# Two attentions and a mixture of experts in one kernel: the steady step's work in another order

## The reference

```python
# layer A: 16 heads of width 8 on ONE shared key and value head, causal, rotary
q = (x @ Wq + bq).reshape(Bx, Tx, 16, 8); k = (x @ Wk + bk)[:, :, None, :]; v = (x @ Wv + bv)[:, :, None, :]
q, k = rope(q), rope(k)
att = softmax(where(causal, -inf, einsum('bthd,bThd->bhtT', q, k) / sqrt(8)))
x = layernorm(x + einsum('bhtT,bThd->bthd', att, v).reshape(...) @ Wo + bo)
# layer B: 16 query heads and 4 key and value heads of width 64, causal, rotary
n = rmsnorm(x, g1); q, k, v = n @ wq, n @ wk, n @ wv ...
h = x + softmax(mask(q k) / 8) v @ wo
# and a mixture of 8 experts (top 2, with a capacity), each gelu((x w2) * (x w1)) w3
x = layernorm(x + h + moe(rmsnorm(h, g2), router_w, router_b, w1, w2, w3))
```

## Time and profile before

| what | value |
|---|---|
| median of the runs | 568.52 us |
| the profiled execution | 569.94 us, of which the span (first to last instruction) 568.1 |
| mean granted TensorE clock over the span | 0.957 of full speed |
| PE busy | 474.3 us (83%), 2980 matmul instructions |
| weight loads busy | 262.4 us (46%) |
| DVE busy | 373.4 us (66%) |
| ACT busy | 231.3 us (41%) |
| POOL busy | 161.9 us (28%) |
| one reduce of a maxima tile on DVE, L1340, mean | 686 ns |
| one copy of a bank by ACT, L1972, mean | 595 ns |

### The profile page before, as it was taken

How to read it: one execution, slowest core, us unless ns; L and a number is a source line. 1 busy time by engine, 2 the same in 40 slices (tenths; PEclk the granted TensorE clock), 3 DMA queues, 4 the chain that set the end, 5 groups by cost and what they waited for, 6 DMA issues and landing times.

```text
span 568.1 us, 8434 instructions
## 1 busy us (share of the span) xinstructions
PE 474.3 (83%) x2980; PEld 262.4 (46%) x2980; DVE 373.4 (66%) x1023; ACT 231.3 (41%) x418; POOL 161.9 (28%) x200
## 2 busy tenths in 40 slices
PE   3877877899899999999998999899888689798730
PEld 2445443454455455536454554455436236465520
DVE  3634789667666786585867577776966136745585
ACT  1252431744554274338334642642431330545332
POOL 4311222402402243033313132232332760051612
PEclk9986999999999999999999999999988789999985
DMA  7400000000030003001100300030430350041213
GB/s 213 168 2 2 1 2 1 2 1 1 3 77 2 0 3 77 1 3 36 42 1 4 76 2 0 5 76 1 141 86 10 106 161 1 1 133 32 64 53 97
DMA packets 19095, 23.95 MB, mean 42 GB/s; under 512 B 2630, under 2 KB 15374, under 8 KB 18158
## 3 DMA queue, kind: packets, MB, share of 16 engines
q1 hardware_dynamic: 15308, 18.29, 11.9%
q0 software_dynamic: 1648, 4.07, 2.6%
q10 hardware_dynamic: 2098, 1.05, 0.6%
HBM read 16.81 MB, written 6.28 MB: 41 GB/s over the span
## 4 chain that ended last, share of the span: by engine, by line
PE 57%; DVE 19%; ACT 11%; issue 6%; POOL 3%; another core or an unknown queue 2%; DMA 1%; ACTq 1%; POOLq 0%; DVEq 0%
PE ps_r L997 6%; PE ps_st L962 6%; PE ps_r L867 5%; DVE rmax_a L1340 4%; ACT pt L1902 4%; PE ps_r L712 4%; PE ps_r L1024 4%; PE ps_st L1242 4%; PE ps_st L951 4%; PE ps_r L1013 3%; PE ps_r L770 3%; DVE rmax L1340 3%; PE ps_r L844 2%; POOL qkr L603 2%
## 5 line engine op out<-in xcount | busy, mean ns | idle before, releaser
L603 POOL TENSOR_TENSOR qkr<-qkr,prod 128x512 f32<-128x512 f32 (+1 forms) x48 | 52.3, 1095 | 191.6 <-DVE prod L1466 190.5
L1340 DVE TENSOR_REDUCE rmax_a<-ps_r 128x2 f32<-128x512 f32 (+1 forms) x96 | 61.2, 686 | 31.2 <-PE ps_r L844 31.0
L1340 DVE TENSOR_REDUCE rmax<-ps_r 128x2 f32<-128x512 f32 (+1 forms) x96 | 60.7, 684 | 13.5 <-PE ps_r L976 13.1
L1902 ACT ACTIVATE pt<-ps_st 128x1024 f32<-128x1024 f32 x48 | 46.5, 1022 | 54.7 <-PE ps_st L754 54.6
L712 PE MATMUL ps_r<-cbt 128*128 128x256 bf16 (+1 forms) x192 | 61.9, 323 | 4.0 <-ACT xT_b L1926 1.1
L1911 ACT ACTIVATE pt<-ps_st 128x1024 f32<-128x1024 f32 x48 | 47.3, 1022 | 37.0 <-PE ps_st L962 31.6
L997 PE MATMUL ps_r<-pt,vb 128*64 128x512 f32 x192 | 50.0, 627 | 7.7 <-issue 4.2
L640 POOL TENSOR_TENSOR oT<-pvb,oT 128x1024 f32<-128x1024 f32 x14 | 32.9, 2371 | 78.9 <-DMA oT<-inv_dram 78.9
L1024 PE MATMUL ps_r<-wqkv,xT_b 128*128 128x512 f32 x96 | 44.5, 600 | 4.3 <-DVE rmax_a L1340 3.5
L712 PEld LDWEIGHTS ps_r<-cbt 128*128 128x128 bf16 x192 | 18.6, 97 | 48.0 <-issue 34.6
L962 PE MATMUL ps_st<-qbuf,kbuf 64*128 64x512 f32 x288 | 39.8, 408 | 0.0
(11 more groups left out here) (238 smaller groups left out, 888.9 us busy)
## 6 DMA issues: line engine op xcount, KB each, us to landing
oT<-inv_dram SPq DMA_DIRECT2D x14, 512.0 KB, 5.7
xs_dram<-pvb SPq DMA_DIRECT2D x1, 2048.0 KB
pt<-in_L_ffn_w SPq DMA_DIRECT2D x2, 1024.0 KB, 7.1
ys_dram<-qkr SPq DMA_DIRECT2D x14, 128.0 KB
qkr<-xs_dram POOLq DMA_DIRECT2D x4, 256.0 KB, 7.0
x_all<-in_L_attn_x ACTq DMA_DIRECT2D x1, 896.0 KB, 7.2
pvb<-xs_dram POOLq DMA_DIRECT2D x3, 256.0 KB, 3.9
out<-x_all SPq DMA_DIRECT2D x1, 640.0 KB
```

The source lines that it names most:

```text
L603: nc.gpsimd.tensor_tensor(part, part, prod[:, (3 * t + i) % 2, 0:w], ALU.add).then_inc(add_in, 1)
L1340: nc.vector.tensor_reduce(heads_of(i), ps_r[:, b, :].rearrange("p (h k) -> p h k", h=4 if i < 4 else 2), AX.X, ALU.max).then_inc(free[b], 1)
L1902: nc.scalar.activation(pt_a(kind)[:, 8 * half:8 * half + 8, :], ps_st[:, c % 2, :, :].rearrange("p b (h t) -> p (b h) t", h=4), ACT.Exp, s ...
```

## The change

The order of a step is another one on all engines, and the ring's list with it; no operation is added or taken away. In PE's stream: `turn_values` and bm0 come ahead of `scores(s, 0)`; the maxima tiles of A and B alternate singly in places; the output projection's two tiles are separated by am6, and stand before bx and bv2; the projection's thirds stand singly between maxima tiles, p12 behind `values_a(s, 0)`; layer A's input is turned earlier; `turn_qk` is split into thirds with `project_a` and `turn_tokens` between. DVE and ACT follow: ACT takes bv3 before the first exponentials of A, DVE rotates p00, p01 and p02 between reduces, and does two splits before `rotate_a`. SP issues the row of nm1 before the sums. Step 7 gets a function of its own on each engine (`last_step`), with the order that it had. The diff, cut (left out are the loops over `range(lo, hi)` in `rotate`, `split` and `high_parts`, and the same calls with all thirds in the opening steps):

```diff
--- before.py
+++ after.py
@@ -68,23 +68,19 @@
 NCH = len(CHUNKS)
-ORDER = [("TA", "tv0"), ("TA", "tv1"), ("MA", "am0"), ("MA", "am1"), ("MB", "bm0"), ("MB", "bm1"),
-         ("TA", "ot0"), ("TA", "ot1"), ("SB", "bv0"), ("MA", "am2"), ("MA", "am3"), ("TA", "ao0"), ("TA", "ao1"),
-         ("MB", "bm2"), ("MB", "bm3"), ("SB", "bv1"), ("SB", "sm0"), ("MA", "am4"), ("MA", "am5"),
-         ("MB", "bm4"), ("MB", "bm5"), ("SB", "bv2"), ("MA", "am6"), ("MA", "am7"), ("MA", "nm0"), ("PB", "bx"),
-         ("TB", "bo0"), ("TB", "bo1"), ("MA", "am8"), ("MA", "am9"), ("MB", "bm6"), ("MB", "bm7"),
-         ("PB", "p00"), ("PB", "p01"), ("PB", "p02"), ("MA", "am10"), ("MA", "am11"), ("SB", "bv3"), ("MA", "nm1"),
-         ("SB", "sm1"), ("MB", "bm8"), ("MB", "bm9"), ("MB", "bm10"), ("MB", "bm11"), ("PB", "p10"), ("PB", "p11"),
-         ("PB", "p12"), ("MB", "nmT"), ("PA", "ax"), ("SA", "av0"), ("PA", "qkv"), ("TB", "xfT"),
-         ("PB", "r00"), ("PB", "r01"), ("PB", "r02"), ("TB", "lg"), ("PB", "r10"), ("PB", "r11"), ("PB", "r12"),
-         ("SA", "av1"), ("PA", "qT0"), ("PA", "qT1"), ("PA", "kT0"), ("PA", "kT1")]
+ORDER = [("TA", "tv0"), ("TA", "tv1"), ("MB", "bm0"), ("MA", "am0"), ("TA", "ot0"), ("TA", "ot1"), ("SB", "bv0"),
+         ("MA", "am1"), ("MA", "am2"), ("MB", "bm1"), ("MA", "am3"), ("SB", "bv1"), ("SB", "sm0"), ("TA", "ao0"),
+         ("TA", "ao1"), ("MB", "bm2"), ("MB", "bm3"), ("MB", "bm4"), ("MB", "bm5"), ("MA", "am4"), ("MA", "am5"),
+         ("MA", "nm0"), ("TB", "bo0"), ("MA", "am6"), ("TB", "bo1"), ("PB", "bx"), ("MA", "am7"), ("SB", "bv2"),
+         ("MA", "am8"), ("MB", "bm6"), ("MB", "bm7"), ("PB", "p00"), ("MA", "am9"), ("PB", "p01"), ("MA", "am10"),
+         ("MA", "am11"), ("SB", "bv3"), ("MB", "bm8"), ("MB", "bm9"), ("MA", "nm1"), ("PB", "p02"), ("SB", "sm1"),
+         ("PA", "ax"), ("MB", "bm10"), ("MB", "bm11"), ("PB", "p10"), ("PB", "p11"), ("MB", "nmT"), ("SA", "av0"),
+         ("PB", "p12"), ("PB", "r00"), ("PB", "r01"), ("PA", "qkv"), ("TB", "xfT"), ("PB", "r02"), ("TB", "lg"),
+         ("PB", "r10"), ("PB", "r11"), ("PB", "r12"), ("SA", "av1"), ("PA", "qT0"), ("PA", "qT1"), ("PA", "kT0"),
+         ("PA", "kT1")]
...
@@ -93,6 +89,9 @@
            + [(FIRST + 2, x) for x in ["ax", "qkv"] + AM[8:] + ["nm1"]],
            NB - 2: [(NB - 2, x) for x in ["bm0", "bm1", "bv0", "bm2", "bm3", "bv1", "sm0", "cnt0", "bm4", "bm5", "bv2"]
         + [f"bm{i}" for i in range(6, 12)] + ["nmT", "rk0", "bo0", "bo1", "bv3", "sm1"]],
+           NB - 1: [(NB - 2, "xfT"), (NB - 1, "bv0"), (NB - 2, "lg"), (NB - 1, "bv1"), (NB - 1, "ws00"), (NB - 1, "ws01"),
+        (NB - 1, "bv2"), (NB, "xg0"), (NB - 1, "ws10"), (NB - 1, "ws11"), (NB - 1, "bv3"),
+        (NB - 1, "bo0"), (NB - 1, "bo1"), (NB, "bo0"), (NB, "bo1")],
...
@@ -537,19 +542,17 @@
     if s == FIRST + 2:
         row_of_max_a(s + 1, 0)
         row_of_max_a(s + 1, 1)
-    if "MA" in on:
-        row_of_max_a(s, 0)
     if s == ROUTED[0]:
         rows_of_max(s)
-    if "SB" in on and s < NB - 1:
-        emptied(sp, s, "sm1")
-        for b in range(2):
-            nc.sync.dma_start(sums[H * b:H * (b + 1), :], smb[RG * b::DB].rearrange("p t c -> p (t c)")) \
-                .then_inc(s_dma, 16)
-    if "MA" in on:
-        row_of_max_a(s, 1)
-    if "MB" in on and s != ROUTED[0]:
-        rows_of_max(s)
+        sums_of_weights(s)
+    elif s < NB - 1:
+        if "MA" in on:
+            row_of_max_a(s, 0)
+            row_of_max_a(s, 1)
+        if "SB" in on:
+            sums_of_weights(s)
+        if "MB" in on:
+            rows_of_max(s)
 sp.wait_ge(oT_in, 1 + NB - 1)
 nc.sync.dma_start(w3s, w3.rearrange("e (k p) c -> p e k c", p=P)).then_inc(w3_in, 16)
...
@@ -854,9 +860,9 @@
     emptied(pe, s, ("am3", "am11")[t])
     nc.tensor.transpose(o[0:H, 0:P], rmax_a[:, H * t:H * (t + 1)], ident).then_inc(full, 1)
-def project_out(s):
-    for t in range(NT):
+def project_out(s, lo, hi):
...
         return
     if s + AHEAD["MB"] == 0:
         pe.wait_ge(prep, 3)
+    if "TA" in on:
+        turn_values(s)
+    maxima(s, 0, 1)
     if "SB" in on:
         pe.wait_ge(n_dma, 32 * (s + 1))
-    scores(s, 0)
-    if s == NB - 1:
-        turn_tokens(NB - 2)
-    if "TA" in on:
-        turn_values(s)
-    maxima_a(s, 0, 2)
-    maxima(s, 0, 2)
+        scores(s, 0)
+    maxima_a(s, 0, 1)
     if "TA" in on:
         turn_out(s)
     if "SB" in on:
         pe.wait_ge(v_in, s + 1)
-    values(s, 0)
-    if s == NB - 1:
-        logits(NB - 2)
-    maxima_a(s, 2, 4)
+        values(s, 0)
+    maxima_a(s, 1, 3)
+    maxima(s, 1, 2)
+    maxima_a(s, 3, 4)
+    values(s, 1)
+    weights(s, 0)
     if "TA" in on:
         project_out_a(s)
     maxima(s, 2, 4)
-    values(s, 1)
-    weights(s, 0)
     scores(s, 1)
+    maxima(s, 4, 6)
     maxima_a(s, 4, 6)
-    maxima(s, 4, 6)
-    values(s, 2)
-    maxima_a(s, 6, 8)
+    scores(s, 2)
     max_rows_a(s, 0)
-    scores(s, 2)
+    if "TB" in on:
+        project_out(s, 0, 1)
+    maxima_a(s, 6, 7)
+    if "TB" in on:
+        project_out(s, 1, 2)
     if "PB" in on:
         pe.wait_ge(xn_in, s + AHEAD["PB"] + 1)
         turn_x(s, "bx", xn)
-    if "TB" in on and s < NB - 1:
-        project_out(s)
-    maxima_a(s, 8, 10)
+    maxima_a(s, 7, 8)
+    values(s, 2)
+    maxima_a(s, 8, 9)
     maxima(s, 6, 8)
     if "PB" in on:
-        project(s, 0)
+        project(s, 0, 0, 1)
+    maxima_a(s, 9, 10)
+    if "PB" in on:
+        project(s, 0, 1, 2)
+    maxima_a(s, 10, 11)
     if "SA" in on:
         scores_a(s, 0)
-    maxima_a(s, 10, 12)
-    if s == NB - 1:
-        turn_slots(0, *GROUPS[0])
-        find_experts(0)
-        weights(s, 1)
-        values(s, 3)
-        project_out(s)
-        project_out(NB)
-    else:
-        values(s, 3)
-        max_rows_a(s, 1)
-        weights(s, 1)
-    maxima(s, 8, 12)
+    maxima_a(s, 11, 12)
+    values(s, 3)
+    maxima(s, 8, 10)
+    max_rows_a(s, 1)
     if "PB" in on:
-        project(s, 1)
+        project(s, 0, 2, 3)
+    weights(s, 1)
+    if "PA" in on:
+        turn_input_a(s)
+    maxima(s, 10, 12)
+    if "PB" in on:
+        project(s, 1, 0, 2)
+    if "MB" in on:
+        max_rows(s)
     if "SA" in on:
         scores_a(s, 1)
-    if "MB" in on:
-        max_rows(s)
-    if "PA" in on:
-        n = s + AHEAD["PA"]
-        turn_x(s, "ax", x_all[:, NT * n:NT * (n + 1), :])
-    if "SA" in on:
         values_a(s, 0)
+    if "PB" in on:
+        project(s, 1, 2, 3)
+        turn_qk(s, 0, 0, 2)
     if "PA" in on:
         project_a(s)
-    if "TB" in on and s < NB - 1:
+    if "TB" in on:
         turn_tokens(s)
     if "PB" in on:
-        turn_qk(s, 0)
+        turn_qk(s, 0, 2, 3)
     if "SA" in on:
         scores_a(s, 2)
-    if "TB" in on and s < NB - 1:
+    if "TB" in on:
         logits(s)
     if "PB" in on:
-        turn_qk(s, 1)
+        turn_qk(s, 1, 0, 3)
     if "SA" in on:
         values_a(s, 1)
     if "PA" in on:
-        turn_qk_a(s)
+        turn_queries_a(s)
+        turn_keys_a(s)
 def turn_slots(n, i, g):
...
         invert(s)
     if "TA" in on:
         normalise_a(s)
-    own_maxima_a(s, 0, 2)
-    maxima(s, 0, 2)
-    if s == NB - 1:
-        take_logits(NB - 2, NB - 3)
-        invert_weights(s, 0)
-        divide_values(s, 0)
-    own_maxima_a(s, 2, 4)
+    maxima(s, 0, 1)
+    own_maxima_a(s, 0, 3)
+    maxima(s, 1, 2)
+    own_maxima_a(s, 3, 4)
     if "TA" in on:
         residual_a(s)
     maxima(s, 2, 4)
     if "TA" in on:
         layernorm_a(s)
     if "PB" in on:
-        x1 = x1_all[:, NT * n:NT * (n + 1), :]
-        if s < 0:
-            normed(n, x1)
-    own_maxima_a(s, 4, 6)
+        normed(n, x1_all[:, NT * n:NT * (n + 1), :])
     maxima(s, 4, 6)
-    if "PB" in on and s >= 0:
-        normed(n, x1)
-    own_maxima_a(s, 6, 8)
-    if s == NB - 1:
-        invert_weights(s, 1)
-        divide_values(s, 1)
+    own_maxima_a(s, 4, 7)
     if "TB" in on:
         residual(s, m)
         mean_square(y, root_t, chain_t, CHAIN_B * m, var_t)
-    own_maxima_a(s, 8, 10)
+    own_maxima_a(s, 7, 9)
     maxima(s, 6, 8)
     if "PB" in on:
-        rotate(s, 0)
+        rotate(s, 0, 0, 1)
+    own_maxima_a(s, 9, 10)
+    if "PB" in on:
+        rotate(s, 0, 1, 2)
     own_maxima_a(s, 10, 12)
+    maxima(s, 8, 9)
     if "TB" in on:
         scaled_tokens(m)
-    maxima(s, 8, 12)
+    maxima(s, 9, 10)
     if "PB" in on:
-        rotate(s, 1)
+        rotate(s, 0, 2, 3)
+    maxima(s, 10, 12)
+    if "PB" in on:
+        rotate(s, 1, 0, 3)
+        split(s, 0, 0, 2)
     if "PA" in on:
         rotate_a(s)
     if "PB" in on:
-        split(s, 0)
-    if "TB" in on and s < NB - 1:
+        split(s, 0, 2, 3)
+    if "TB" in on:
         take_logits(s, m)
     if "PB" in on:
-        split(s, 1)
+        split(s, 1, 0, 3)
...
-    if s == NB - 1:
-        turned_tokens(NB - 2)
     if "TA" in on:
         take_turned(s)
     take_values(s, 0)
+    take_values(s, 1)
+    take_weights(s, 0)
     if "TA" in on:
```

(37 more changed lines are left out.)

123 lines of the change are left out of this document (88 added, 35 removed).

## The result

The changed kernel takes 547.46 us (median of four runs, 546.69 to 549.79), the kernel before beside it 568.14 (four runs, 567.76 to 568.71): ratio 0.9664, 95% interval 0.9628 to 0.9701, a gain of 20.7 us. The forecast was 551.9, the range 546.5 to 562.0: faster, as said, and 4.4 us better.

The account below looks back on a forecast made before the run. PE's instruction stream bounds a step, through waits and order. Steps 1 to 3 -9.7, 0 -2.6, 4 -3.1, 5 -2.0, -1 -1.0: -18.4, plus 1.8 allowance, -16.6: profiled 569.94 to 553.3, median 551.9 us; range 546.5 to 562.

Parts of the forecast that it names:

- The full steps' sum: Steps 1 to 3 together: 158.2 to 148.5 us, -9.7, at 49.5 us a full step.
- The price of the borders: Full step on PE: 8 more borders beside projection tiles and output projection halves, 0.05 us each on the mean, 0.4 us.
- the walk: List of PE's start times in a full step of the new order, checked against bank releases; end at 49.5 us.
- The allowance of +0.3 a step: Seven gates (starts hanging on a bank's release) clear by under 0.2 us; for those that fail, +1.8 us in all.
- The same edit's part for av0 and qkv: PE's waits before av0 and qkv, 0.57 and 0.45 us in brackets, go since p12, r00 and r01 stand about them.
- Steps 0, 4 and 5: Step 0 47.68 to 45.1 us, step 4 49.99 to 46.9, step 5 40.16 to 38.1: -2.6, -3.1, -2.0.
- The waits kept: Step 4: 0.8 us for av1's exponentials; step 5: 0.75 at its start, 1.4 in its tail for rotations and splits.
- The scaling of block A's variance: On VectorE at about 11.6 us, inside GpSimd's second half: 1.3 us lost there, PE 0.1 at most.
- Waits back elsewhere: Rival: with VectorE 0.5 us later, four gates fail before r12; full steps gain 1.3, not 3.2; 560.5 us; 18%.
- Borders dear: Rival: each of 8 new borders bares a weight load and matmul tail, 3.6 us more a step; 571.5 us; 6%.
- Given back behind step 5: Rival: steps 6 and 7 lose clock or wait for the load of w1 and w2; 568.5 us if all; 6%.
- Row of maxima late: Rival: the row's transfer lands beyond scores_a 1's 1.6 us margin; 3.3 us late means 569 and over; 4%.

Follow-up runs that it names:

- edit 5: Turned queries and keys split by thirds, rotate_a behind two splits; undone in the changed kernel: 548.77 us, ratio 0.9745 to the kernel before.
- Edit 1: turn_values and bm0 ahead of scores 0; undone in the changed kernel: 536.93 us, ratio 0.9648 to the kernel before.
- Edit 2: Output projection split around am6, before bx, values 2 behind; undone in the changed kernel: 545.01 us, ratio 0.9797 to the kernel before.
- Edit 3: Projection thirds between single maxima; undone for projection 0 only, in the changed kernel: 541.09 us, ratio 0.975 to the kernel before.
- Edit 4: ScalarE takes bv3 before block A's first two exponentials; undone in the changed kernel: 548.58 us, ratio 0.9675 to the kernel before.
- second profile of the kernel before: The kernel before the change run again, nothing edited: 557.2 us, ratio 1.0039 to the kernel before.
- edit 2 alone: The kernel before with only the output projection moved ahead of am6 and bx, values 2 behind: 559.94 us, ratio 0.9884 to the kernel before.
- ax behind nmT: The changed kernel with the turned block-A input back behind the turned maxima: 549.53 us, ratio 0.9666 to the kernel before.
- the second comparison: The changed kernel run again, nothing edited, beside the kernel before: 543.76 us for 562.83, ratio 0.9703.
- the open ends: The changed kernel with the third split ahead of rotate_a in steps -1 and 0, and scores 0 ahead of turn_values in step 5: 544.69 us, ratio 0.9698.

## Why the prediction was right, and where it was off

The mechanism was right: PE's stream sets the step, the waits go one by one, nothing takes their place in a full step but one at r12. The undone edits cost 2.0 (the half clock left out), 6.5, 5.5, 0.3 and 3.4 us, 17.7 together (0.8 of it GpSimd's hold in step 1 without edit 5), and the change brings 18.3 in the same steps: nearly all of it is told by edits undone one at a time. That the two sums are so close is in part luck, since ax's move is in none of the five, and it and edit 5 cover the same two waits, at av0 and qkv.

- *The full steps' sum, forecast -9.7.* 158.20 to 147.19 us, -11.0. Two terms were too dear. The price of the borders, 0.4 us a step, is hardly there: the walk gave a single third 0.95 us, and it takes 0.86; a full step without its wait is 49.03 - 0.37 = 48.66 us, where the estimate for the stream was 48.5. And r12 waits 0.37 for 0.55.
- *The allowance of +0.3 a step for gates that fail.* None failed: 49.0 measured, 49.5 walked, 49.8 with the allowance. These 1.8 us and the 1.3 above are the core of the miss: in steps -1 to 5 the forecast had 16.6 and the runs have 19.65.
- *Edit 1, 0.6 us a full step.* 0.37 by undoing it. The wait that the kernel before had was as large as forecast: bv0 started 0.89 us behind turn_out in step 2 (218.53 to 219.42) and starts 0.31 behind it now, 0.58 less; but in the new ring the old place costs less than it did. Its price at the start of step 5 is 0.80 in the bracket, 0.95 with a handover, for 0.75 forecast with it.
- *Edit 2, 0.96 us.* Alone it brings 1.05, and its removal costs 1.1 to 1.4: in the new order bx and am7 wait too, which the term didn't hold.
- *Edit 3, the nm1 part 0.72 us.* The wait came back on undoing it, at 1.0 to 1.3 us a step, so the term was too small: nm1 starts 0.85 us later in step 2 (32.59 for 31.74), p10 0.87 (36.55 for 35.68), against the 0.72 that I took.
- *The same edit's part for av0 and qkv, 1.3 us.* They went, but "since p12, r00 and r01 stand about them" is only one of two reasons, each enough by itself: with these put back the waits stayed away, and with only ax put back as well. The walk carried ax at its new place, ahead of bm10, and I gave that no term.
- *Edit 4, nothing.* 0.3 us over six steps, all in one whose products began late.
- *Steps 0, 4 and 5, forecast -2.6, -3.1 and -2.0.* Measured -2.65, -2.8 and -1.9; the wait at the start of step 5 lies in step 4's window here, so the last two are to be read together: 4.65 for 5.1. The waits kept are not those of the sum: step 4 has 0.15 and 0.38 us in brackets for 0.8, step 5 has 0.80 at its start, 0.44, 0.47 and 0.16 in its tail for 1.4, and 0.31 before its last scores, for an exponential, which the sum didn't hold. Which of them makes the 0.4 us was not tried. *Step -1, forecast -1.0*: -1.34 at full clock. One wait there and in step 0 I did not see: av1 waits 0.98 us for the split behind the rotation, as no logits stand between.
- *GpSimd and VectorE.* The scaling of block A's variance was forecast at 11.6 us of the step, to lose 1.3. In the timeline of DVE in step 2, with POOL's products (212.69, 4.69 long) ending at 217.38:

```profile
216.12 1.28 DVE L1453 TENSOR_SCALAR root_a_v<-mv 128x2 f32<-128x2 f32 x1
217.32 0.15 DVE L1454 TENSOR_SCALAR root_a_v<-mv 128x2 f32<-128x2 f32 x1
```

It starts at 11.5, takes 1.28 and ends with the product; the one behind takes 0.15. The Trainium skill, SBUF — State Buffer, Who interferes with whom, says that of the two the later is blocked; the trace agrees. bo0 didn't wait for it: it started at 17.89 us, as walked. What I missed is that the price hangs on the start: DVE's operation there took 0.53 us at 223.48 in step 2 of the kernel before and 1.72 at 170.26 in step 1, where the step was 0.74 us longer than the next. PE has a wait in that step which it doesn't have in steps 2 and 3, before values 2, whose bank is am4's:

```profile
176.59 1.94 PE L997 MATMUL ps_r<-pt,vb 128*64 128x512 f32 x8 [0.67 <-DVE rmax_a L1340]
```

In the second profile of the kernel before the products began at 10.3 us of step 1 for 9.6; this wait is 1.40 us there, and the step 1.5 us longer than the next. With edit 2 alone they began at 8.2, the wait is not there, and step 1 takes 51.4 us as steps 2 and 3 do. So the 0.7 us by which step 1 gains more than step 2 (4.2 for 3.5) is this wait. Whether it went because the products began earlier (8.3) or because values 2 stands elsewhere now is open, since no run changed their start by itself; but a late start still costs in the new order: 0.3 us at 8.65 (step 2 with edit 4 undone), 0.3 at 8.68 (step 3 with ax behind nmT), 0.8 at 9.12 (step 1 with edit 5 undone).

- *The rivals.* Waits back elsewhere: no. Borders dear: no, 0 for the one measured and 0.16 us at most for all eight (48.66 - 48.5); the 0.3 us for a matmul's tail in that rival's price stands in no row. The one entry into a tiled block less, 0.1 us in the prediction, is below what these sums can tell. Given back behind step 5: no, the pairs on one chip show that stretch to vary without regard to the change. Row of maxima late: no wait on a transfer stands before scores_a 1.

What stays open: the sum of steps -1 to 5 at full clock is 19.65 us and the medians differ by 20.7; the second comparison gave 19.1 (562.83 to 543.76). The intervals of the two comparisons are gains of 17.0 to 21.1 and 13.6 to 19.9 us. 19.65 lies in both, so I claim no more than that for the change.

## What to carry to other kernels

Where one engine's stream sets the time, write down its start times for the new order and compare each with the time at which its buffer comes free: here that walk was within 0.5 us in 49 and named the one wait that came in a full step; it missed the 0.98 us in steps -1 and 0, which have no logits. Walk what you measured, not an allowance on top; and give every moved instruction its own line in the account, since the one left out (ax) was enough by itself to remove two of the waits. Moving a wait's cause away from one user only helps if no other user stands right behind it, as the attempt to close the open ends shows.

## What the runs showed of the hardware

- The granted clock of step -1 is not the same from run to run: 1.00 in eleven of the fourteen profiles, 0.95 in three, and for the changed kernel one of each. In that step TensorE waits 3.1 us for `xn`, in the profiles at either clock, so the wait alone doesn't decide it; of the projection behind, four matmuls then take 3.21 us in the first profile of the changed kernel, at a granted clock of 0.50 from 91 to 94 us (1.2 of 2.4 GHz), and 1.96 in the second. With edit 1 undone the clock was 0.50 at the end of step 5 and cost 0.8 us.
- The time behind step 5 varies between 144 and 160 us for programs that are the same there. From the first to the second scores of step 7 it is 7.6 us in all four runs on one chip and 15.1 to 17.0 on the others. The trace doesn't say what PE waits for there: where a row has an idle time, it names issue (4.09 us) or exponentials.
- An operation of two elements a partition on VectorE took 0.53, 1.28, 1.72 or 2.34 us, by where GpSimd's two products stood when it began: up to the whole of one (4.71 for two). A delay of 1 us in their start, which comes with the return of the sums from DRAM, made a step 0.8 us longer with edit 5 undone, and in the second profile of the kernel before, where they began 1.6 us later in step 1 than in step 2, step 1 is 1.5 us longer.
- Idle time in brackets understates what a wait costs: 0.18 for 0.37 before r12, and none for the 0.31 us of edit 1. Pitches between starts, beside the same pitch undisturbed, give it.
